# Local layers' output product: four f32 products per tile become twelve f32r products, attention's output being split beforehand

## The chip, the cores and the metric

One core of a Trainium2 chip runs the whole program. The metric is the device time of one execution in microseconds (us). Engines are named as the profile names them: PE is TensorE's matmul, PEld its weight loads, DVE is VectorE, ACT is ScalarE, POOL is GpSimd, SP is SyncE, which here only issues transfers.

## The reference, cut to what matters

A global attention over x (4 x 1024 tokens, 256 features, 16 heads) gives a gate. A second branch takes the normalised x through two layers of local attention and a gated feed-forward net; the two are multiplied and x is added. Of a local layer this case touches one line, `x = x + o  wo`:

```python
def _layer(x, wqkv, qs, ksc, wo, lg, lb, w1, b1, w2, b2):
    h = shift_token(x)
    q, k, v = jnp.split(h  wqkv, 3, axis=-1)
    ...
    o = local_attention(q, k, v)              # 8 heads of 64, windows of 128
    o = o.transpose(0, 2, 1, 3).reshape(b, n, INNER)   # INNER = 512
    x = x + o  wo                            # wo: 512 x 256 per layer
    h = shift_token(x)
    ...                                       # layer norm
    a, g = jnp.split(h  w1 + b1, 2, axis=-1)
    x = x + (a * gelu(g))  w2 + b2
    return x
```

## The kernel before

Three stages follow each other, with a barrier between them. `prepare_tokens` normalises x and makes the queries, keys and values of the global attention. `global_attention` works on 32 units; early in it SP also brings in what the local layers need: it copies the raw wqkv and w1 from DRAM to DRAM (`copy_raw`, L820 and L821), then issues `place_rows` (the row maxima that the first score products of the stage need, L437), then the small tables, `load_wo`, `load_w2`, waits for the raw copies, and issues `load_wqkv` and `load_w1`. `local_layers` is the long stage.

In `local_layers` the 4096 tokens are 8 chunks of 512 columns, each chunk four windows of 128. `body(g)` runs for g = 0 to 17 on every engine; the list `PLAN` fixes which layer's attention and which layer's feed-forward it does. In body(g), window w, the attention of chunk g is prepared (`project`, `rotate`), scored one window later and weighted with the values another window later, while the feed-forward net of chunk g - 2 goes on in parts between them. Bodies 0 and 1 have no feed-forward part; in its place they do the output projection of the global attention (`divide`, `project_o`, `take_s`). Bodies 3 to 7, 8 and 9, and 11 to 15 are hardware loops. Bodies 2 to 16 hold 15 output products and the last chunk's one is written out apart (`late_output`, in body 16). There is no scheduler: each engine executes its function in the order in which it is written, and semaphores alone tie them together. So the order around the change is that of the functions `body` of each engine.

What is touched: the output product (`output_product`, `late_output`) reads the attention's output from `o_ring` (two slots of 4 x 512 columns, f32) and the weights from `wo_l`, as f32 operands: 4 matmuls for each of the two output tiles m. `o_ring` is filled by ScalarE from the bank `l_ps_o` in `take_o` (L1474); a chunk's slot is complete after window 1 of the next body, and the product reads it in window 0 of the body after that. Other large products of the local layers already are f32r: their operands were split into a high part (rounded to f32r) and a low part (the remainder), and three products high x high, low x high, high x low stand for one (`THREE`). The feed-forward net's features are kept so in `f_high` and `f_low` (512 columns x 2 each), the projection's in `h`. `exponentials` (ScalarE) goes through the 8 heads of a window, four per half; `normalise` (VectorE, L1688) scales them; `add_ffn` (VectorE, L1774) empties the banks of the `down` product, ffn1 and then ffn0, which the next output product fills again, and `carry` (L1780) ends VectorE's part of a body. `scale_tables` (VectorE, L1888) multiplies a layer's rope tables by its scales: layer 0 ahead of body 0, layer 1 in window 1 of body 2.

## Time and profile before

| | |
|---|---|
| time, median of 3 runs | 2290.24 us (2288.89 to 2292.75) |
| the profiled execution's own time | 2290.47 us |
| its span in the trace | 2287.5 us |
| mean granted TensorE clock in it | 0.975 of full |
| PE busy | 2176.3 us (95%) |
| DVE busy | 1630.8 us (71%) |
| ACT busy | 1375.2 us (60%) |
| POOL busy | 614.8 us (27%) |

Busy time is the time in which an engine had an instruction under way. In the rows below, a body is named by its number, and a line is that of the kernel before. A row of the timeline gives the start, the duration and the instruction, and in square brackets how long its engine stood idle before it and who released it. An f32 matmul of 512 columns stands in the trace as two records, an f32r matmul as one: "x16" of the output product is 8 matmuls.

### The profile page before, as it was taken

Reading aid. Unit: us, or ns where it says so; the run is one execution under the profiler, and the core shown is the slowest. Engines: PE = TensorE matmul, PEld = TensorE weight load, DVE = VectorE, ACT = ScalarE, POOL = GpSimd, SP = SyncE. Lnnn points to the kernel's source line nnn. Section 1 sums busy time; section 2 is a strip of 40 time slices with the busy share of each in tenths; the row PEclk is TensorE's granted clock in tenths of the full one; section 3 lists DMA queues with packets and bytes.
Section 4 is the critical chain, followed back from the end, with each engine's and each line's share of the span. In section 5 each row is a group of like instructions: output and inputs, shape, how many; then the busy total and the mean of one; then the engine's idle time right before and its main releaser. Section 6 shows DMA issues by size and latency. Waiting matters only on the chain.

```text
span 2287.5 us, 43380 instructions
## 1 busy us (share of the span) xinstructions
PE 2176.3 (95%) x14560; PEld 1278.4 (56%) x14560; DVE 1630.8 (71%) x3801; ACT 1375.2 (60%) x2547; POOL 614.8 (27%) x493
## 2 busy tenths in 40 slices
PE   7869999999999988989999999999999999999998
PEld 4533333333333335656766766756766766766755
DVE  6668999999999936666666665656666666665645
ACT  2215888888888864645655655645655655655633
POOL 4421200000000005423333333323333333333302
PEclk9977999999999999999999999999999999999999
DMA  4485222112211122210000000000010000000122
GB/s 149 172 240 175 57 67 62 55 55 66 66 57 54 38 63 95 95 38 1 1 0 0 0 0 0 28 1 1 9 37 1 1 0 0 0 0 0 55 92 74
DMA packets 76983, 108.94 MB, mean 48 GB/s; under 512 B 14204, under 2 KB 49360, under 8 KB 76752
## 3 DMA queue, kind: packets, MB, share of 16 engines
q1 hardware_dynamic: 76864, 107.30, 14.9%
q8 instruction: 81, 1.33, 0.2%
q14 instruction: 38, 0.31, 0.0%
HBM read 68.74 MB, written 43.95 MB: 49 GB/s over the span
## 4 chain that ended last, share of the span: by engine, by line
PE 50%; DVE 2%; issue 2%; ACT 1%; DVEq 0%; ACTq 0%
PE ffn L1201 24%; PE l_ps_o L1159 5%; PE ring L1147 5%; PE ring L1187 4%; PE ps_v L1134 3%; PE ps_q L1134 3%; PE ring L1171 2%; PE ps_k L1134 2%; DVE l_probs L1676 1%; PE ring L1189 1%; PE ring L1190 0%; DVE l_probs L1688 0%; ACT k_ring L1482 0%; ACT l_probs L1490 0%; PE ps_k L1223 0%
## 5 line engine op out<-in xcount | busy, mean ns | idle before, releaser
L669 DVE TENSOR_REDUCE maxima<-ps_m 128x1 f32<-128x512 f32 x1024 | 629.3, 683 | 22.5 <-PE ps_m L549 18.2
L737 ACT ACTIVATE probs<-ps_st 128x1024 f32<-128x1024 f32 x512 | 521.0, 1024 | 163.8 <-PE ps_st L576 144.8
L549 PE MATMUL ps_m<-k_st,q_st 48*128 48x512 f32 x1024 | 394.0, 468 | 19.9 <-DMA k_st<-ks 15.8
L1490 ACT ACTIVATE l_probs<-l_probs,l_neg_max 128x256 f32<-128x256 f32 x512 | 254.0, 498 | 194.6 <-DVE l_neg_max L1676 194.6
L576 PE MATMUL ps_st<-q_st,k_st 50*128 50x512 f32 x1024 | 369.1, 445 | 1.2 <-DMA q_st<-max_rows 0.9
L592 PE MATMUL ps_o<-probs,v_st 128*32 128x256 f32 x4096 | 323.4, 394 | 0.1
L1676 DVE CUSTOM_DVE_ANT_1 l_probs<-ring,l_mask 128x256 f32<-128x256 f32 x384 | 140.0, 421 | 198.6 <-PE ring L1187 198.2
L576 PEld LDWEIGHTS ps_st<-q_st,k_st 50*128 50x128 f32 x1024 | 155.1, 187 | 194.4 <-issue 174.9
L1469 ACT COPY p_turned<-ring 128x512 f32<-128x512 f32 x256 | 140.5, 599 | 163.5 <-PE ring L1147 163.3
L1096 POOL TENSOR_SCALAR clipped<-sumsq 128x16 f32<-128x16 f32 x64 | 16.2, 253 | 767.4 <-DVE sumsq L1643 767.4
L549 PEld LDWEIGHTS ps_m<-k_st,q_st 48*128 48x128 f32 x1024 | 167.4, 191 | 53.3 <-DVE maxima L669 31.3
L1098 POOL TENSOR_TENSOR inv_norm<-clipped,halves 128x16 f32<-128x16 f32 x64 | 187.6, 2932 | 5.3
L592 PEld LDWEIGHTS ps_o<-probs,v_st 128*32 128x32 f32 x4096 | 84.3, 108 | 170.5 <-ACT probs L737 110.4
L1769 DVE SCALAR_TENSOR_TENSOR hidden<-ffn,b_l,gate 128x512 f32<-128x512 f32 x96 | 71.9, 749 | 144.0 <-PE ffn L1201 69.7
L1201 PE MATMUL ffn<-hidden,w_l 128*128 128x512 f32 x384 | 172.9, 600 | 0.0
L1688 DVE TENSOR_SCALAR l_probs<-l_probs,l_inv_total 128x256 f32<-128x256 f32 x512 | 166.3, 388 | 4.5
L1147 PE MATMUL ring<-l_ident,l_probs 128*128 128x128 f32 x1024 | 143.5, 281 | 14.4 <-DVE l_probs L1688 14.4
L1100 POOL TENSOR_TENSOR rope_a<-rope_a,rope_b 128x1024 f32<-128x1024 f32 x64 | 156.9, 2452 | 0.0
L1159 PE MATMUL l_ps_o<-p_turned,v_ring 128*64 128x128 f32 x2048 | 149.1, 283 | 4.6 <-ACT p_turned L1469 4.5
L508 POOL TENSOR_TENSOR max_hl<-row_max,zeros 128x16 fp32r<-128x16 f32 x32 | 7.1, 223 | 532.8 <-DVE row_max L678 532.8
L1159 PEld LDWEIGHTS l_ps_o<-p_turned,v_ring 128*64 128x64 f32 x2048 | 109.4, 137 | 65.6 <-issue 42.0
L1106 POOL TENSOR_TENSOR qk_n<-rope_a,inv_norm 128x1024 f32<-128x1024 f32 x64 | 123.2, 1926 | 72.7 <-PE ring L1171 62.4
(192 smaller groups left out, 3868.9 us busy)
## 6 DMA issues: line engine op xcount, KB each, us to landing
qs<-split SPq DMA_DIRECT2D x16, 512.0 KB, 3.5
ks<-split SPq DMA_DIRECT2D x16, 512.0 KB, 5.1
q_st<-qs SPq DMA_DIRECT2D x64, 128.0 KB, 2.6
k_st<-ks SPq DMA_DIRECT2D x64, 128.0 KB, 3.2
o<-o_sb SPq DMA_DIRECT2D x32, 256.0 KB, 2.5
hidden<-o SPq DMA_DIRECT2D x17, 256.0 KB, 6.1
x_in<-in_L_attn_x_dram SPq DMA_DIRECT2D x8, 512.0 KB, 5.6
v<-v_sb SPq DMA_DIRECT2D x16, 256.0 KB, 4.7
```

The lines of the kernel that those rows point to most:

```text
L549: nc.tensor.matmul(bank(base, use)[:, :], q_st[u][r, qt * P:(qt + 1) * P], k_st[u][r, h * CH:(h + 1) * CH], start=True, stop=True).then_in ...
L576: mm = nc.tensor.matmul(ps_st[j][:, h * CH:(h + 1) * CH], k_st[u][r, kt * P:(kt + 1) * P], q_st[u][r, h * CH:(h + 1) * CH], start=True, st ...
L592: mm = nc.tensor.matmul(ps_o[r:r + 32, q], v_st[:, kt, 2 * u + j, :], probs[:, kt % 4, j, h * CH + q.start:h * CH + q.stop], start=(kt == ...
L669: nc.vector.tensor_reduce(maxima[:, par, side(e), tile + e // 4, e % 2:e % 2 + 1], bank(base, k + e)[:, :], AX_X, ALU.max).then_inc(m_used, 1)
L737: nc.scalar.activation(probs[:, kt % 4, j, :], ps_st[j][:, :], ACT.Exp, scale=float(G_DIM) ** -0.5).then_inc(exp_done, 1)
L1098: nc.gpsimd.tensor_tensor(inv_norm[:, :], clipped[:, :], halves[:, :], ALU.pow).then_inc(inv_done, 1)
L1134: mm = nc.tensor.matmul(bank[:, :], h[a][:, k, w * P:(w + 1) * P], wt.wqkv[b][:, k, n * INNER:(n + 1) * INNER], start=(e == 0), stop=(e == ...
L1147: mm = nc.tensor.transpose(ring[(PT + p) % 2][:, (2 * j + s) * P:(2 * j + s + 1) * P], probs[:, 2 * p + j, s * P:(s + 1) * P], wt.ident[:, :])
L1159: mm = nc.tensor.matmul(ps_o[j * HDIM:(j + 1) * HDIM, p * P:(p + 1) * P], v_ring[:, slot, head * HDIM:(head + 1) * HDIM], p_turned[:, p % ...
L1201: mm = nc.tensor.matmul(ffn[bank][:, :], a, b, start=(n == 0), stop=(n == len(operands) - 1))
L1490: nc.scalar.activation(probs[:, head, :], probs[:, head, :], ACT.Exp, bias=neg_max[:, head:head + 1], scale=-1.0, accum_out=total[:, head: ...
L1688: ins = nc.vector.tensor_scalar(probs[:, head, :], probs[:, head, :], inv_total[:, head:head + 1], None, ALU.mult)
```

## The change

`wo` is held twice, high and low (f32r), and o_ring's room is shared with a new tile `o_low` (f32r) of the same size and place. In window 3 of body g (g = 1 to 15) ScalarE copies the slot that body g + 1 will multiply into `f_high` and `f_low`, which are free then: columns of heads 0 to 3 into f_high, 4 to 7 into f_low (`take_o_high`, 2 copies of 128 x 1024, between the two halves of the exponentials). GpSimd then subtracts that from o_ring, in place (`leave_o_low`, 2 operations of 128 x 1024). The output product takes 12 f32r matmuls per tile m in place of 4 f32 ones and waits for GpSimd (`o_split`) instead of ScalarE (`o_out`). For the last chunk the same is done in window 1 of body 16, into the tiles h.

The weights: SP copies wo raw from DRAM to DRAM too, ahead of `place_rows`, waits for three copies instead of two, and loads wo after w1. Ahead of bodies 2 and 10 ScalarE rounds wo into the high tile and VectorE subtracts; PE waits for that (`wo_low`) before the body's first product. For room, the `scales` now lie in `rope_a`, so both layers' tables are scaled ahead of body 0 and none in body 2.

```diff
 global_attention, sync
                 wt.copy_raw(sp)
                 place_rows(0, 0)
                 wt.load_small(nc, sp)
-                wt.load_wo(sp, 0)
                 wt.load_w2(sp, 0)
-                sp.wait_ge(wt.raw, 32)
+                sp.wait_ge(wt.raw, 48)
                 wt.load_wqkv(sp, 0)
                 wt.load_w1(sp, 0)
+                wt.load_wo(sp, 0)
...
+        sp.dma_start(self.wo_dram, self.dram["wo"]).then_inc(self.raw, 16)
...
-        scales = sb("scales", [P, DEPTH, 2, HDIM])
+        scales = rope_a[:, 0, 0:DEPTH * 2 * HDIM].rearrange("p (l s n) -> p l s n", l=DEPTH, s=2)
...
+        def o_high(g, p):
+            return features_of(g)[p // KD][:, p % KD, :]
+
+        def wo_products(g, m):
+            low = o_low[:, g % 2, :, :] if isinstance(g, int) else o_low[:, bass.ds(g % 2, 1), :, :].rearrange("p o h n -> p (o h) n")
+            cols = slice(m * P, (m + 1) * P)
+            return [(wt.wo[a][:, p, cols], low[:, p, :] if b else o_high(g, p)) for p in range(HEADS // 2) for a, b in ((0, 0), (1, 0), (0, 1))]
...
+                if weights and weights[0] == "w1" and prepare:
+                    prepare("wo", weights[1])
 gpsimd
+                def leave_o_low(g):
+                    pool.wait_ge(o_high_done, g - 1)
+                    slot = (lambda x: x[:, g % 2, :, :]) if isinstance(g, int) else (lambda x: x[:, bass.ds(g % 2, 1), :, :].rearrange("p o h n -> p (o h) n"))
+                    for p in range(0, HEADS // 2, KD):
+                        ins = nc.gpsimd.tensor_tensor(slot(o_low)[:, p:p + KD, :], slot(o_ring)[:, p:p + KD, :], features_of(g)[p // KD][:, :, :], ALU.subtract)
+                    ins.then_inc(o_split, 1)
...
+                        if isinstance(g, int) and g == LAST and w == 1:
+                            leave_o_low(g + 1)
...
+                        if w == 3 and not (isinstance(g, int) and g == 0):
+                            leave_o_low(g + 1)
 tensor
                 def output_product(g, lf):
-                    pe.wait_ge(o_out, WPC * (g - 1))
+                    pe.wait_ge(o_split, g - 1)
                     for m in range(KD):
-                        ffn_fill(g, m, WO, [(wt.wo[:, p, m * P:(m + 1) * P], o_ring[:, bass.ds(g % 2, 1), p, :].rearrange("p o n -> p (o n)"))
-                                            for p in range(HEADS // 2)])
+                        ffn_fill(g, m, WO, wo_products(g, m))
...
                         if w == 0 and before_hidden:
-                            pe.wait_ge(wt.wo_in, 16 * (lf + 1))
+                            pe.wait_ge(wt.wo_low, lf + 1)
 scalar
+                def take_o_high(g):
+                    act.wait_ge(o_out, WPC * (g - 1))
...
+                    for p in range(0, HEADS // 2, KD):
+                        ins = nc.scalar.copy(features_of(g)[p // KD][:, :, :], slot[:, p:p + KD, :])
+                    ins.then_inc(o_high_done, 1)
...
                         if mid_:
-                            exponentials(W)
+                            exponentials(W, (lambda: take_o_high(g + 1)) if split_next else None)
+                        if isinstance(g, int) and g == LAST and w == 1:
+                            take_o_high(g + 1)
...
+                    if name == "wo":
+                        act.wait_ge(wt.wo_in, 16 * (l + 1))
+                        nc.scalar.copy(wt.wo[0][:, :, :], wt.wo[1][:, :, :].bitcast(F32)).then_inc(wt.wo_high, 1)
+                        return
 vector
+                    if name == "wo":
+                        dve.wait_ge(wt.wo_high, l + 1)
+                        nc.vector.tensor_tensor(wt.wo[1][:, :, :], wt.wo[1][:, :, :].bitcast(F32), wt.wo[0][:, :, :], ALU.subtract).then_inc(wt.wo_low, 1)
+                        return
                     if l == 0:
-                        scale_tables(0 if name == "wqkv" else 1)
+                        if name == "wqkv":
+                            for layer in range(DEPTH):
+                                scale_tables(layer)
                         return
```

What stands on the engines, in the order of the compiled programs. PE, the loop of bodies 3 to 7, start of the output product in window 0, before (line 1201; ISA and REGISTER_ALU rows compute an address or a wait's value):

```order
L1245 ISA
L1197 ISA [waits o_out]
L1201 ISA [waits ffn_taken0]
L1201 MATMUL ffn<-o_ring,wo_l 128x512
L1201 ISA
L1201 MATMUL ffn<-o_ring,wo_l 128x512
L1201 ISA
L1201 MATMUL ffn<-o_ring,wo_l 128x512
L1201 ISA
```

The same place now (line 1233):

```order
L1277 REGISTER_ALU
L1229 ISA [waits o_split]
L1233 MATMUL ffn<-f_high,wo_high 128x512 [waits ffn_taken0]
L1233 MATMUL ffn<-f_high,wo_low 128x512
L1233 ISA
L1233 MATMUL ffn<-o_low,wo_high 128x512
L1233 MATMUL ffn<-f_high,wo_high 128x512
L1233 MATMUL ffn<-f_high,wo_low 128x512
L1233 ISA
```

The product keeps its place between the turned probabilities and the values. Its wait is for GpSimd's signal now, and a tile's 4 matmuls are 12, with four address computations still among the first tile's.

ACT, same loop, window 3, now (line 1534 is that of the exponentials, 1523 that of the new copies): the last three of the first half's four exponentials, then the copies.

```order
L1534 ACTIVATE l_probs,l_total<-l_probs,l_neg_max 128x256
L1534 ACTIVATE l_probs,l_total<-l_probs,l_neg_max 128x256 [waits ring_taken1]
L1534 ACTIVATE l_probs,l_total<-l_probs,l_neg_max 128x256
L1523 ISA [waits o_out]
L1523 COPY f_high<-o_ring 128x1024
L1523 ISA
L1523 COPY f_low<-o_ring 128x1024
L1533 REGISTER_ALU
```

The second half's exponentials, which followed the first half's directly, now come behind both copies.

And POOL, same loop, window 3, now: the sum and the multiplication of the window (lines 1130 and 1136), then the subtractions (1113).

```order
L1130 TENSOR_TENSOR rope_a<-rope_a,rope_b 128x1024
...
L1136 TENSOR_TENSOR qk_n<-rope_a,inv_norm 128x1024 [waits ring_ready1]
L1113 ISA [waits o_high_done]
L1113 TENSOR_TENSOR o_low<-o_ring,f_high 128x1024
L1113 ISA
L1113 TENSOR_TENSOR o_low<-o_ring,f_low 128x1024
L1081 REGISTER_ALU
```

Before, the loop ended behind the multiplication into qk_n; the two subtractions are new there.

## Rows read from the trace of the kernel before

**Rows 1.** The page: the span.
```profile
span 2287.5 us, 43380 instructions
```
**Rows 2.** Busy by stretch, body 5: length; PE, PEld, DVE, ACT, POOL; granted clock.
```profile
1251.40:1335.30 83.90, 82.89 (x489) 56.51 (x489) 53.29 (x153) 48.47 (x119) 30.08 (x16) 1.00 0.00 0
```
**Rows 3.** The chain that ended last, 1228 to 1320: start, us, what.
```profile
1251.40 6.87 PE ffn L1201 x16
...
1312.58 2.81 PE ffn L1201 x12
```
**Rows 4.** Timeline, 1228 to 1290: window 3 of body 4 into body 5.
```profile
1243.37 0.51 ACT L1490 ACTIVATE l_probs<-l_probs,l_neg_max 128x256 f32<-128x256 f32 x1 [3.95 <-DVE l_neg_max L1676]
...
1245.69 1.14 DVE L1688 TENSOR_SCALAR l_probs<-l_probs,l_inv_total 128x256 f32<-128x256 f32 x4
...
1247.77 0.75 DVE L1774 SCALAR_TENSOR_TENSOR xnt<-ffn,b_l,mid 128x512 f32 x1 [0.28 <-PE ffn L1201]
...
1251.23 7.03 PE L1201 MATMUL ffn<-o_ring,wo_l 128*128 x16
```
**Rows 5.** Timelines of POOL and of DVE around 1286, window 1 of body 5.
```profile
1285.48 1.91 POOL L1106 TENSOR_TENSOR qk_n<-rope_a,inv_norm 128x1024 f32<-128x1024 f32 x1 [0.23 <-POOL rope_a L1100]
...
1285.78 2.55 DVE L1688 TENSOR_SCALAR l_probs<-l_probs,l_inv_total 128x256 f32<-128x256 f32 x4
```
**Rows 6.** Groups by line and form: busy us, mean ns.
```profile
L870 POOL TENSOR_TENSOR wqkv_low<-wqkv_low,wqkv_high 128x1536 fp32r<-128x1536 f32 x2 | 6.9, 3474 | 0.2
...
L1610 ACT CAST wqkv_high<-wqkv_low 128x1536 fp32r<-128x1536 f32 x2 | 2.8, 1460 | 0.0
```
**Rows 7.** Transfers by line: KB each, us from issue to landing.
```profile
w_raw<-in_L_ffn_w_dram SPq DMA_DIRECT2D x1, 2728.0 KB, 21.5
```
**Rows 8.** Timeline, 160 to 212: the first score product of the global stage.
```profile
184.74 0.79 PE L576 MATMUL ps_st<-q_st,k_st 50*128 50x512 f32 x1 [0.87 <-DMA q_st<-max_rows]
```
**Rows 9.** Timeline, 832 to 860: start of the local stage.
```profile
851.97 2.63 DVE L1888 TENSOR_TENSOR tables<-tables,scales 128x512 f32<-128x512 f32 x6 [4.58 <-DMA scales<-in_L_ffn_k_scale_dram]
...
858.56 0.60 PE L1134 MATMUL ps_q<-wqkv_high,h_high 128*128 128x512 f32 x1 [4.58 <-DVE rope_b L1648]
```
**Rows 10.** Timeline, 972 to 987: window 3 of body 1.
```profile
984.80 1.22 DVE L1655 TENSOR_TENSOR mid<-hidden 128x1024 f32<-128x1024 f32 x1
...
986.08 1.22 PE L1284 MATMUL ffn<-mid,dev 128*128 128x512 f32 x1 [5.74 <-DVE mid L1655]
```
**Rows 11.** Timeline of PE, 990 to 1032: body 2's start and its window 1.
```profile
993.39 0.47 PE L1134 MATMUL ps_q<-wqkv_high,h_high 128*128 128x512 f32 x1 [0.72 <-issue]
...
1030.83 0.50 PE L1189 MATMUL ring<-k_ring,q_t 64*128 64x128 f32 x4 [1.87 <-DVE l_neg_max L1676]
```
**Rows 12.** Timeline, 1493 to 1512: body 7 into body 8.
```profile
1500.94 3.43 DVE L1877 TENSOR_TENSOR wqkv_low<-wqkv_low,wqkv_high 128x1536 fp32r<-128x1536 f32 x2
...
1504.70 0.79 PE L1134 MATMUL ps_q<-wqkv_high,h_high 128*128 128x512 f32 x1 [5.17 <-DVE wqkv_low L1877]
...
1511.24 1.02 PE L1201 MATMUL ffn<-o_ring,wo_l 128*128 x2
```
**Rows 13.** Timelines of PE and DVE, 1668 to 1680: body 9 into body 10.
```profile
1675.04 0.79 PE L1134 MATMUL ps_q<-wqkv_high,h_high 128*128 128x512 f32 x1
...
1676.89 0.23 DVE L1780 TENSOR_SCALAR xnt<-xnt,parity  x1 [0.50 <-DVE xnt L1774]
...
1679.11 1.45 PE L1201 MATMUL ffn<-o_ring,wo_l 128*128 128x512 f32 x3
```
**Rows 14.** Timeline of PE, 2186 to 2287: body 16.
```profile
2203.84 1.97 PE L1147 MATMUL ring<-l_ident,l_probs 128*128 128x128 f32 x8 [2.42 <-DVE l_probs L1688]
...
2214.67 0.40 PE L1201 MATMUL ffn<-f_high,w_high 128*128 128x512 f32 x1
```
**Rows 15.** Busy by stretch, same columns: the two us behind that wait.
```profile
2204.00:2206.00 2.00, 1.81 (x8) 1.41 (x8) 1.77 (x8) 1.97 (x5) 0.00 (x0) 0.50 0.00 0
```
**Rows 16.** Timeline of ACT, 2196 to 2287: body 16, windows 1 and 2.
```profile
2213.78 0.69 ACT L1534 ACTIVATE gate<-ffn,b_l 128x512 f32<-128x512 f32 x1
```

More of the change, by code:

```diff
@@ L783, in __init__ @@
         self.w1 = [sb(f"w1_{n}", [P, KD, (2 * FT + 1) * P], F32R) for n in ("high", "low")]
-        self.wo = sb("wo_l", [P, INNER // P, D])
+        self.wo = [sb(f"wo_{n}", [P, INNER // P, D], F32R) for n in ("high", "low")]
         self.w2 = sb("w2_l", [P, FT + 1, D])
@@ L797, in __init__ @@
         self.w1_dram = nc.dram_tensor("w1_raw", (DEPTH, D, 2 * HID), F32, kind="Internal").ap()
+        self.wo_dram = nc.dram_tensor("wo_raw", (DEPTH, INNER, D), F32, kind="Internal").ap()
         self.raw = sem("raw")
@@ L800, in __init__ @@
         self.w1_high, self.w1_low = sem("w1_high"), sem("w1_low")
+        self.wo_high, self.wo_low = sem("wo_high"), sem("wo_low")
         self.set = sem("w_set")
@@ L914, in local_layers @@
         p_turned = sb("p_turned", [P, 2, 2, 2, P])
-        o_ring = sb("o_ring", [P, 2, HEADS // 2, CH])
+        with nc.sbuf_tensor("o_ring", [P, 2, HEADS // 2, CH], F32) as o_ring:
+            pass
+        o_low = sb("o_low", [P, 2, HEADS // 2, CH], F32R)
         mid = sb("mid", [P, KD, 1 + CH])
@@ L957, in local_layers @@
         sq_dev = sem("sq_dev")
+        o_high_done, o_split = sem("o_high_done"), sem("o_split")
         mid_summed = sem("mid_summed")
@@ L1227, in late_output @@
                     g = LAST + 1
-                    pe.wait_ge(o_out, WPC * (g - 1))
+                    pe.wait_ge(o_split, g - 1)
                     pe.wait_ge(roped, WPC * LAST)
                     for m in range(KD):
-                        late_fill(m, [(wt.wo[:, p, m * P:(m + 1) * P], o_ring[:, g % 2, p, :]) for p in range(HEADS // 2)])
+                        late_fill(m, wo_products(g, m))
                 def late_mean():
@@ L1243, in output_product @@
                 def output_product(g, lf):
[L1245 removed]
+                    pe.wait_ge(o_split, g - 1)
                     for m in range(KD):
[L1247 to L1248 removed]
+                        ffn_fill(g, m, WO, wo_products(g, m))
                 def mean(g):
@@ L1482, in take_qk, with exponentials @@
                     nc.scalar.copy(k_ring[:, :, ws * P:(ws + 1) * P], ring[TK % 2][:, :].rearrange("p (h n) -> p h n", n=P)).then_inc(ring_taken[TK % 2], 1)
-                def exponentials(W):
+                def take_o_high(g):
+                    act.wait_ge(o_out, WPC * (g - 1))
+                    if late(g):
+                        act.wait_ge(v_mm, WPC * LAST)
+                    slot = o_ring[:, g % 2, :, :] if isinstance(g, int) else o_ring[:, bass.ds(g % 2, 1), :, :].rearrange("p o h n -> p (o h) n")
+                    for p in range(0, HEADS // 2, KD):
+                        ins = nc.scalar.copy(features_of(g)[p // KD][:, :, :], slot[:, p:p + KD, :])
+                    ins.then_inc(o_high_done, 1)
+                def exponentials(W, between=None):
                     for n in range(HEADS):
+                        if n == HEADS // 2 and between:
+                            between()
                         head = scored(n)
@@ L1583, in body @@
                             take_s(W - 1)
+                        split_next = w == 3 and not (isinstance(g, int) and (g == 0 or g >= LAST))
                         if mid_:
-                            exponentials(W)
+                            exponentials(W, (lambda: take_o_high(g + 1)) if split_next else None)
+                        if isinstance(g, int) and g == LAST and w == 1:
+                            take_o_high(g + 1)
                         if not forward and W == CHUNKS - 1:
```

5 lines of the change are left out of this document (2 added, 3 removed).

## Prediction

> **What bounds the kernel now.** I read the page first: a span of 2287.5 us [rows 1]. The profiled execution's own time, 2290.47 us, is 2.97 more, and 0.23 above the median 2290.24. The sum below is made against 2290.47. Next, busy time by stretch: in one body of the steady part, 83.90 us long, PE is busy for 82.89, DVE for 53.29, ACT for 48.47 and POOL for 30.08, at full granted clock [rows 2]. The reader should see that PE is the bound there and that the others have room, though not at every moment. Then the chain that ended last: in the steady bodies it stays on PE, an output product takes 6.87 us in it and a hidden tile of 12 f32r matmuls 2.81 [rows 3]. Last, the timelines of the places where PE does stand idle, because there the bound is another engine: the starts of the stages [rows 8, 9], the end of body 1 [rows 10], body 8's start [rows 12], body 16 [rows 14].
>
> **The gain.** One f32r matmul of this size costs 2.81 / 12 = 0.234 us [rows 3]. The new product has 24 of them: 5.62 us in place of 6.87, 1.25 saved. There are 15 output products and the late one: 16 x 1.25 = 20.0 us, all of it PE time. PE is at full clock around nearly all of them.
>
> **The steady border (bodies 3 and up), costed at nothing.** ScalarE's two copies: a cast of 1536 columns takes 1.46 us [rows 6], so 1024 take 0.97 and both 1.95. They stand where ACT idles for 3.95 us until VectorE's maxima of the second half [rows 4]; with that cover gone they would cost 1.95 a border. GpSimd's two subtractions: the only row of that form gives 3.47 us for 1536 columns [rows 6], so 2.31 each, 4.63 together. They start when the copies end, at about 1241.4, and end at 1246.0 to 1246.5. Is VectorE free meanwhile? In window 1 of body 5 a group of four `normalise` operations, begun while POOL ran qk_n until 1287.39, took 2.55 us instead of 1.14 [rows 4, 5]. So I hold VectorE's operations that touch SBUF alone until GpSimd's instruction ends; without that hold the sum below would be 5.8 us lower (2.4 in c, 1.7 in e, 1.7 in f). The Trainium skill (page "SBUF — State Buffer", section "SBUF: two separate sides") has this as a rule that speaks against the change: GpSimd and VectorE share a port pair that whoever starts first locks for its whole instruction. By that rule, the trace agrees: the whole excess of the row is one stay until qk_n's end, and a mere sharing of bandwidth would have the sum near the lower one. With the hold, both groups of normalise end at about 1248.9 where the second ended at 1246.8, and `add_ffn` of bank ffn0, before 1247.77 + 0.75 = 1248.5, ends at about 1250.4. The output product needs that bank at 1251.23 [rows 4]: 0.9 us are left, so I charge nothing. `carry` comes 1.7 later, and it only matters where something behind it is awaited (below). Queued behind PE's new wait for `o_split` are the whole window's products, but GpSimd is done 4.7 us before it.
>
> **The losses, in order of time.**
> a. The raw copy of wo, 1024 KB, is ahead of `place_rows` in SP's queue. The raw copies of wqkv (2 x 256 x 1536 x 4 bytes = 3072 KB) and of w1 (2728 KB) are in after 21.5 us [rows 7], so 1024 KB more take at most 21.5 x 1024 / 5800 = 3.8 us. PE's first score product waits for the transfer that `place_rows` makes [rows 8]. Other transfers share those 21.5 us, so I take +3.0 (0, if the rows pass beside the copies, to 3.8). The load of wo, moved behind w1, lands long before the local stage.
> b. Layer 1's tables are scaled ahead of body 0 too: VectorE's 2.63 us [rows 9] lie straight on the path to `rope_b` and PE's 4.58 of idle. +2.65. In body 2's window 1 they go, and with them PE's wait of 1.87 for VectorE's maxima [rows 11]: -1.9.
> c. End of body 1. ACT's exponentials of the two halves are back to back here (no wait between them), so the copies push the second half back by 1.95; the last ended at 983.4. The subtractions run from about 983.3 to 987.9 and hold normalise and `divide` (1.22 us, from 984.80), for which PE stands idle until 986.08 [rows 10]. Divide would end at 987.9 + 1.14 + 1.22 = 990.3 against 986.0: +4.4 (2.0, if GpSimd holds nothing, to 4.6).
> d. Body 2's start. PE waits for `wo_low` before its first product: ScalarE, once done with the last `take_s` (about when PE starts), rounds wo in 0.97, VectorE subtracts in 3.43 / 2 x 2 / 3 = 1.15 [rows 12], 0.15 of signals: +2.25, since PE now goes on at once [rows 11]. What does an idle of that kind do to the clock? After 2.42 us of idle at 2203.84 the granted clock was 0.50, the level of 1.2 GHz [rows 14, 15]. After body 8's 5.17 the way from the first product to the output product took 6.54 us, against 4.07 in body 10: 2.5 lost [rows 12, 13]. Bounds 0 and 3.4; an idle of 2.25 is nearest to the 2.42, but short: +1.5.
> e. Body 8's start hangs on VectorE: carry, then 3.43 us for wqkv, then PE [rows 12]. Carry 1.7 later: +1.7 (0 to 2.3).
> f. Body 10's start. Before, PE went on at 1675.04. Now it waits until carry (1677.12), 1.15 of subtraction and 0.15 of signal are over, 1678.4: +3.4. Carry's delay adds 1.7 (0 to 2.3), and the clock 2.4 as at body 8 (0 to 2.9) [rows 12, 13]. Together +7.5.
> g. Body 16. The copies for the last chunk stand ahead of ACT's gate 0 (2213.78 to 2214.47) [rows 16], whose bank PE refills at 2214.67 [rows 14]: 1.95 later, +1.85. An idle of that length may lower the clock: +0.8 (0 to 1.7). The subtractions are done long before the late product.
>
> Sum: 3.0 + 0.75 + 4.4 + 3.75 + 1.7 + 7.5 + 2.65 = 23.75; less 20.0, +3.75: 2294.2 us, 2294.0 against the median.
>
> **The rivals.**
> Faster: GpSimd does not hold VectorE here, and the clock does not fall. For it: VectorE may slip in between GpSimd's two instructions, and the idles of d and g are shorter than any behind which my rows show a fallen clock. Against it: [rows 5, 12, 15]. The terms c, e and f lose 2.4, 1.7 and 1.7, the clock 1.5, 2.4 and 0.8: 10.5 less, 2283.7, or 2283.5 against the median.
> Slower: the border is dearer than I think, so that ffn0 comes free after PE asks for it. It decides from 0.9 us on: if the copies take 1.4 us each, or a subtraction 2.8, every one of some 13 borders stalls. With a stall of 0.7 us each, +9: about 2303. For it: my 2.31 is scaled from an instruction outside the loop, and the slack is the smallest in the argument. Against it: POOL's sum over 1024 columns takes about the same (qk_n 1.91 [rows 5]).
> The change does not do what it says: the f32r product is no faster, because the address computations that stand between the first tile's matmuls stop the flow, as an f32 matmul's length hid them. At 0.06 to 0.25 us for each of four, in 12 looped products, +3 to +12: 2297 to 2306, say 2300 (with four times 0.12). Against it: the hidden tiles run at 0.234 though they too are in the loops, but with few such computations between.
>
> **How the numbers follow.** The forecast case, terms near my values, has 0.52; its own range is 2289.5 to 2298.5, from the two or three terms that can be off at once. Faster has 0.20, the slow border 0.13, the stopped flow 0.07; 0.08 stays for what I have not seen, half to each side. The measurement tells some 0.2% (4.6 us) from no change, so faster is below 2285.7 and slower above 2294.8. My case is half under and half over the upper bound with most of its weight under it (0.34 to 0.18); so faster 0.20 + 0.04, slower 0.13 + 0.07 + 0.18 + 0.02, same 0.36. The range 2283 to 2302 reaches into the faster case and to the slow border, leaving about a tenth at either end.
>
> **What would show it.** In the profile after: an output product of 24 matmuls in 5.6 us in the chain (a product above 6 means the flow is stopped); POOL's new operations near 2.31 and ACT's copies near 0.97; the normalise groups of window 3 twice as long as 1.14; no idle of PE before the output product, by ffn0's release. PE idle of about 5 us before the first products of bodies 2 (2.2) and 10 (5), half the clock behind them; at the global stage's start a first score product 3 us later, counted from the stage's barrier; project_o's last wait near 10 us. I would be wrong by the largest amount if body 10's start costs only its 3.4, or if each border stalls a little: the number of borders multiplies whatever I have missed there.

## The result, and the profile after

The changed kernel takes 2306.99 us (median of 5 runs, 2305.39 to 2315.7), the kernel before 2289.68 us beside it (5 runs, 2287.88 to 2292.75). The ratio on record is 1.0065, 95% interval 1.0046 to 1.0084; the quotient of the two medians, 1.0076, lies inside it. The change makes the kernel slower, by 13 us more than forecast (2294.0), and the time lies above the range (2283 to 2302).

The page of the changed kernel: the span grew by 17.6 us, though PE has 15 us less to do (2161.2 us of busy time against 2176.3 in the table above).

```profile
span 2305.1 us, 43754 instructions
...
PE 2161.2 (94%) x14688; PEld 1303.6 (57%) x14688; DVE 1673.2 (73%) x3803; ACT 1406.7 (61%) x2581; POOL 689.3 (30%) x525
```

Where is the difference? The starts of a body's first PE product in both traces give it stage by stage (body 0 by its window 1):

| | before | after | behind | grown by |
|---|---|---|---|---|
| first score product, global stage | 184.74 | 189.16 | 4.42 | 4.42 |
| last score product of that stage | 840.27 | 844.59 | 4.32 | -0.10 |
| body 0, window 1 | 858.56 | 865.82 | 7.26 | 2.94 |
| body 1 | 914.75 | 922.24 | 7.49 | 0.23 |
| body 2 | 993.39 | 1006.84 | 13.45 | 5.96 |
| body 3 | 1079.29 | 1091.30 | 12.01 | -1.44 |
| body 7 | 1415.03 | 1426.23 | 11.20 | -0.81 |
| body 8 | 1504.70 | 1517.02 | 12.32 | 1.12 |
| body 9 | 1591.10 | 1602.34 | 11.24 | -1.08 |
| body 10 | 1675.04 | 1690.73 | 15.69 | 4.45 |
| body 11 | 1762.95 | 1780.25 | 17.30 | 1.61 |
| body 15 | 2098.70 | 2115.50 | 16.80 | -0.50 |
| last instruction of DVE | 2283.50 | 2301.01 | 17.51 | 0.71 |

The steps up at the edges are there much as forecast. What is missing are the steps down: bodies 3 to 6 and 11 to 14 should have gained 1.25 us each and gained 0.8 and 0.5 in four together.

So I looked into one steady body. PE's timeline of the changed kernel, body 5:

```profile
1262.61 0.48 PE L1233 MATMUL ffn<-f_high,wo_high 128*128 128x512 f32 x1
...
1268.34 1.09 PE L1191 MATMUL l_ps_o<-p_turned,v_ring 128*64 128x128 f32 x16
1269.37 1.09 PE L1179 MATMUL ring<-l_ident,l_probs 128*128 128x128 f32 x8
1271.40 1.10 PE L1233 MATMUL ffn<-hidden,mean_w 128*128 128x512 f32 x2 [0.94 <-issue]
```

The product is as short as forecast: from its start to the next step 5.73 us (1262.61 to 1268.34), where it took 6.96 (1251.23 [rows 4] to 1258.19, below). There is no wait ahead of it in this body. But three steps on, before the product that forms the mean of `mid`, PE is idle for 0.94 us. "Issue" hides the releaser; the mean's operand is VectorE's sum (L1782), so I read VectorE next, same kernel and place:

```profile
1255.60 3.00 DVE L1739 TENSOR_SCALAR l_probs<-l_probs,l_inv_total 128x256 f32<-128x256 f32 x4
...
1259.79 1.40 DVE L1825 SCALAR_TENSOR_TENSOR xnt<-ffn,b_l,mid 128x512 f32 x2
...
1268.56 0.69 DVE L1756 TENSOR_TENSOR mid<-ffn,xnt 128x512 f32<-128x512 f32 x1 [1.07 <-PE ffn L1233]
1269.35 1.95 DVE L1782 TENSOR_TENSOR hidden<-mid 128x512 f32<-128x512 f32 x1
```

And GpSimd:

```profile
1253.00 2.36 POOL L1113 TENSOR_TENSOR o_low<-o_ring,f_high 128x1024 f32 x1 [2.17 <-ACT f_low L1523]
1255.31 2.36 POOL L1113 TENSOR_TENSOR o_low<-o_ring,f_low 128x1024 f32 x1
1265.15 0.25 POOL L1126 TENSOR_SCALAR clipped<-sumsq 128x16 f32<-128x16 f32 x1 [7.48 <-DVE sumsq L1694]
...
1268.39 2.37 POOL L1130 TENSOR_TENSOR rope_a<-rope_a,rope_b 128x1024 f32<-128x1024 f32 x1
```

The sum takes 1.95 us, and it ends 0.54 us after GpSimd's addition does (1270.76), a little less than the 0.69 us that it takes when it runs freely. The same three instructions in the timeline of the kernel before, and the step behind its output product:

```profile
1256.55 2.35 POOL L1100 TENSOR_TENSOR rope_a<-rope_a,rope_b 128x1024 f32<-128x1024 f32 x1
...
1258.19 1.09 PE L1159 MATMUL l_ps_o<-p_turned,v_ring 128*64 128x128 f32 x16
1259.21 0.69 DVE L1731 TENSOR_TENSOR hidden<-mid 128x512 f32<-128x512 f32 x1
...
1260.15 1.02 PE L1201 MATMUL ffn<-hidden,mean_w 128*128 128x512 f32 x2
```

There the addition ended at 1258.90 and the sum began 0.31 us later, untouched. The reader should see that 0.31 us: it was all the room between the two. The output product, now 1.3 us shorter, brings the sum forward by as much, into the addition.

Bodies 2 to 15 all show it, in two sizes. In bodies 4 to 7, 9 and 12 to 15 GpSimd's addition also begins 0.38 to 0.55 us later, counted from the body's start, than before, and PE's idle ahead of the mean is 0.94 to 1.11 us. In bodies 3 and 11 the addition begins 9.39 us after the start, as it did before; the sum then takes 1.56 us and the idle is 0.56 us (in bodies 2, 8 and 10 it is 0.56 to 0.61). Body 3, which begins at 1091.30:

```profile
1100.69 2.37 POOL L1130 TENSOR_TENSOR rope_a<-rope_a,rope_b 128x1024 f32<-128x1024 f32 x1
...
1102.04 1.56 DVE L1782 TENSOR_TENSOR hidden<-mid 128x512 f32<-128x512 f32 x1
...
1103.71 1.10 PE L1233 MATMUL ffn<-hidden,mean_w 128*128 128x512 f32 x2 [0.56 <-issue]
```

Over the 14 bodies this idle adds up to 12.1 us; the kernel before has none there.

The other main places where PE idles in the changed kernel, one for each of the terms a to g, in their order, and between f and g one more, for which the prediction has no term:

```profile
189.16 0.79 PE L576 MATMUL ps_st<-q_st,k_st 50*128 50x512 f32 x1 [4.86 <-DMA q_st<-max_rows]
...
865.82 0.80 PE L1166 MATMUL ps_q<-wqkv_high,h_high 128*128 128x512 f32 x1 [7.51 <-DVE rope_b L1699]
...
997.54 2.93 PE L1315 MATMUL ffn<-mid,dev 128*128 128x512 f32 x3 [9.70 <-DVE mid L1706]
...
1006.84 0.80 PE L1166 MATMUL ps_q<-wqkv_high,h_high 128*128 128x512 f32 x1 [2.88 <-DVE wo_low L1923]
...
1517.02 0.79 PE L1166 MATMUL ps_q<-wqkv_high,h_high 128*128 128x512 f32 x1 [6.40 <-DVE wqkv_low L1934]
...
1690.73 0.80 PE L1166 MATMUL ps_q<-wqkv_high,h_high 128*128 128x512 f32 x1 [3.98 <-DVE wo_low L1923]
...
2202.12 0.47 PE L1233 MATMUL ffn<-f_high,wo_high 128*128 128x512 f32 x1 [1.29 <-DVE xnt L1825]
...
2233.41 0.50 PE L1233 MATMUL ffn<-f_high,w_high 128*128 128x512 f32 x1 [1.71 <-ACT gate L1578]
```

The row at 2202.12 is body 16's output product. PE has no new chunk to project ahead of it there, comes to it early, and waits for `add_ffn` (L1825) to empty the bank. The kernel before shows no such wait in body 16; all kernels below that hold the change show one of 1.28 or 1.29 us.

### The profile page after: what moved, and what is told of

Same layout as the page of the kernel before. It is cut to its first block and busy times, and to the rows that moved or that the text cites. A ratio compares the mean times of both kernels' runs of the same rounds, so it can differ in the third digit from the quotient of the medians.

```text
span 2305.1 us, 43754 instructions
## 1 busy us (share of the span) xinstructions
PE 2161.2 (94%) x14688; PEld 1303.6 (57%) x14688; DVE 1673.2 (73%) x3803; ACT 1406.7 (61%) x2581; POOL 689.3 (30%) x525
## 3 DMA queue, kind: packets, MB, share of 16 engines
q8 instruction: 82, 1.34, 0.3%
## 5 line engine op out<-in xcount | busy, mean ns | idle before, releaser
L737 ACT ACTIVATE probs<-ps_st 128x1024 f32<-128x1024 f32 x512 | 520.8, 1024 | 167.9 <-PE ps_st L576 148.6
L1739 DVE TENSOR_SCALAR l_probs<-l_probs,l_inv_total 128x256 f32<-128x256 f32 x512 | 193.9, 441 | 4.5
```

The source lines that it names most:

```text
L737: nc.scalar.activation(probs[:, kt % 4, j, :], ps_st[j][:, :], ACT.Exp, scale=float(G_DIM) ** -0.5).then_inc(exp_done, 1)
L1739: ins = nc.vector.tensor_scalar(probs[:, head, :], probs[:, head, :], inv_total[:, head:head + 1], None, ALU.mult)
```

## The experiments

Ten kernels, on two groups of questions: what takes the gain of the steady bodies, and what the edges cost. Beside them the kernel before was timed on the same chip, with medians of 2293 to 2294 us. Between the traces most of the difference that no edit explains arises in one place: at the start of the global stage the granted clock rises from 0.50 to full at different moments. In the stretch 200 to 230 us it was 0.53 on the mean in wait_late and 1.00 in raw_later, and that stage then lasted 663.6 and 652.8 us from its first to its last score product. So the steady bodies are compared by their period in the traces, the distance from the first product of body 5 to that of body 6; in a trace it repeats from body 4 to body 6 within 0.15 us.

**pool_waits.** GpSimd's addition behind VectorE's sum, in window 0.

```diff
                         pool.wait_ge(roped, W + 1)
+                        if w == 0 and lf is not None:
+                            pool.wait_ge(mid_summed, g - 1)
                         nc.gpsimd.tensor_tensor(rope_a
```

> The changed kernel, but GpSimd starts the addition of the rotated parts in window 0 (L1130) only after VectorE's sum for the mean (L1782). In the changed kernel that sum took 1.95 us in body 5, ending about when the addition does, and PE then stood idle 0.94 us before the mean's product; PE was 1.31 us ahead of the old schedule before that product and 1.10 of it was gone after. Theory (GpSimd's addition holds VectorE's sum, and the shorter output product brings the sum into it): the sum takes 0.69 us again, the idle goes, and each of 13 bodies gains 1.0 to 1.25 us: 13 to 16 us less than the changed kernel's 2307, 2291 to 2294. Rival (the sum is late for another reason, the delay of VectorE at the border or the product's own end): the sum stays near 1.95 us or PE waits as long, and the time stays within 3 us of 2307. GpSimd's later addition should cost nothing, as it waits 3.9 us for PE's turn behind it.

Measured: 2297.57 us (10 runs), ratio to the kernel before 1.0004 (0.9984 to 1.0024). The period fell from 83.80 to 82.64, 1.16 us. VectorE and GpSimd in body 5:

```profile
1273.19 0.69 DVE L1758 TENSOR_TENSOR mid<-ffn,xnt 128x512 f32<-128x512 f32 x1 [1.06 <-PE ffn L1235]
1273.99 0.69 DVE L1784 TENSOR_TENSOR hidden<-mid 128x512 f32<-128x512 f32 x1
...
1274.76 2.36 POOL L1132 TENSOR_TENSOR rope_a<-rope_a,rope_b 128x1024 f32<-128x1024 f32 x1 [1.70 <-DVE hidden L1784]
```

The sum takes 0.69 us as soon as the addition is not beside it, and PE goes on to the mean at once. The addition, 1.7 us later, costs nothing that the period shows. The theory holds; the time in us stands above the expected 2291 to 2294, but the kernel before, timed beside it, took 2293.55 us, 3.9 more than beside the changed kernel. By the ratios, 1.0004 against 1.0065, the wait gives back some 0.6%, 14 us.

**mean_later.** The same stall, covered instead of removed.

```diff
-                        if forward and w == 0 and not late(g):
-                            mean(g)
...
                             values(W, w, 3)
+                        if forward and w == 0 and not late(g):
+                            mean(g)
```

> The changed kernel, but PE does the mean's product behind the last two products with the values of window 0 (1.03 us of work) in place of ahead of them; GpSimd and VectorE keep their order. Theory (PE waits only for the sum, held by GpSimd until its addition ends): the sum still takes about 1.95 us, but PE's idle of 0.94 before the mean is filled, and 0.9 to 1.0 us a body are gained in 13 bodies, some 12 us: about 2295. Rival (the whole chain behind the mean, centring, squares, variance, has no room, so that the stall only moves): PE idles later in the window, and the time stays within 3 us of 2307.

Measured: 2299.13 us (10 runs), ratio 1.0009 (0.9981 to 1.0037); period 83.06, 0.74 us less than the changed kernel's, where 0.9 to 1.0 was expected, and 0.42 us more than with pool_waits. The sum still takes 1.95 us in its median, and PE no longer waits for it. So most of what PE lost was the wait for the sum. Part of the rest is a new wait, for ScalarE's copy of the turned probabilities, ahead of the products that were moved forward:

```profile
1277.71 1.15 PE L1191 MATMUL l_ps_o<-p_turned,v_ring 128*64 128x128 f32 x16 [0.24 <-ACT p_turned L1500]
```

The other 0.2 us is not accounted for.

**before_short.** The kernel before with a shorter output product and nothing of the change.

```diff
-                                            for p in range(HEADS // 2)])
+                                            for p in range(HEADS // 2 - 1)])
```

> The kernel before, with one of the four f32 matmuls of each output tile left out (its output leaves out heads 6 and 7 in the output product). No operation of the change is in it. An output product is 6.87 / 4 = 1.72 us shorter. Theory (a shorter output product alone brings VectorE's sum into GpSimd's addition, which ends 11.7 us after the body's start whatever PE does): the sum waits for it, takes up to about 2 us, and PE is only 0.3 to 0.6 us ahead per body behind the mean; the time falls by 16 x 0.3 to 0.6, 5 to 10 us below the kernel before. Rival (the copies and subtractions of the change are what makes VectorE or GpSimd late): without them the full 1.72 us a product comes through, 16 x 1.72 = 27 us below the kernel before.

Measured: 2281.85 us (10 runs), ratio 0.9952 (0.9934 to 0.9969). The period is 83.42 against 83.94: of 1.72 us taken off PE, 0.52 arrive. Body 5's start in its timeline:

```profile
1263.77 2.36 POOL L1100 TENSOR_TENSOR rope_a<-rope_a,rope_b 128x1024 f32<-128x1024 f32 x1
...
1263.92 0.69 DVE L1705 TENSOR_TENSOR mid<-ffn,xnt 128x512 f32<-128x512 f32 x1 [1.04 <-PE ffn L1201]
1264.72 1.96 DVE L1731 TENSOR_TENSOR hidden<-mid 128x512 f32<-128x512 f32 x1
...
1266.79 1.10 PE L1201 MATMUL ffn<-hidden,mean_w 128*128 128x512 f32 x2 [0.95 <-issue]
```

No copy, no subtraction, no f32r product: the shorter product alone brings the sum into the addition. The rival, that the stall needs the change's own operations, is out. (This product is 1.72 us shorter, not 1.31, so the sum begins 0.95 us into the addition, and the idle is as long as in the changed kernel's later additions. How much of the changed kernel's own stall comes from the shorter product alone is read from its bodies 3 and 11: 0.56 us. The time is 11.7 us below the kernel before, where the expectation had 5 to 10; 3.7 of them arise behind body 15's start.) The first DVE row is worth a look too: the addition to `mid`, which reads a PSUM bank, ran 0.69 us beside GpSimd, unheld.

**short_waits.** before_short with the wait of pool_waits.

```diff
-                                            for p in range(HEADS // 2)])
+                                            for p in range(HEADS // 2 - 1)])
...
+                        if w == 0 and lf is not None:
+                            pool.wait_ge(mid_summed, g - 1)
```

> The kernel before with one of four f32 matmuls of each output tile left out (heads 6 and 7 are missing from the output product, as in before_short) and GpSimd's addition of window 0 behind VectorE's sum. Nothing of the change is in it. Theory: what the shorter product gave back in before_short (period 83.43 instead of 83.94, 0.51 of 1.72 us) comes through: period 82.2 to 82.3, and 13 to 15 us less than before_short, 1.1 to 1.2% below the kernel before. Rival (the stall behind the shorter product has a second cause): the period stays above 82.8.

Measured: 2266.52 us (4 runs), ratio 0.9876 (0.9848 to 0.9905). The period is 82.23: the 1.72 us arrive whole (1.71), and there is no second cause behind the first. GpSimd's wait by itself gains nothing either, or more than 1.72 would have arrived.

**add_halves.** Is it a hold, or do the two engines share a rate?

```diff
-                        nc.gpsimd.tensor_tensor(rope_a[:, :, :], rope_a[:, :, :], rope_b[:, :, :], ALU.add).then_inc(added, 1)
+                        for s in range(2):
+                            ins = nc.gpsimd.tensor_tensor(rope_a[:, s, :], rope_a[:, s, :], rope_b[:, s, :], ALU.add)
+                        ins.then_inc(added, 1)
```

> The changed kernel, but GpSimd's addition of the rotated parts is two instructions of 512 columns in place of one of 1024, in every window. It tells what is held and for how long. Theory (VectorE's instruction on SBUF alone stands still until the GpSimd instruction under way ends): VectorE's sum for the mean, begun 0.9 to 1.0 us into the addition, is let in at the first half's end, some 0.3 us later, and takes 0.9 to 1.2 us instead of 1.95; GpSimd's second half then starts later or beside it; PE's idle before the mean falls from 0.94 to 0.1 or less, and a looped body takes 82.7 to 83.1 instead of 83.8 to 83.95 us. Rival (the two engines only share the rate): the sum still takes 1.8 to 2.0 us, since the same amount of GpSimd's work lies beside it, and the bodies keep their period.

Measured: 2297.9 us in one run; the period is 82.87 in place of 83.80. The timeline of body 5:

```profile
1265.90 1.27 POOL L1131 TENSOR_TENSOR rope_a<-rope_a,rope_b 128x512 f32<-128x512 f32 x1
...
1267.13 1.72 POOL L1131 TENSOR_TENSOR rope_a<-rope_a,rope_b 128x512 f32<-128x512 f32 x1
...
1266.86 0.86 DVE L1784 TENSOR_TENSOR hidden<-mid 128x512 f32<-128x512 f32 x1
...
1267.82 1.10 PE L1235 MATMUL ffn<-hidden,mean_w 128*128 128x512 f32 x2
```

The sum began 0.96 us into the first half and took 0.86 us, a little below the expected 0.9. It ended 0.55 us after the first half's end (1267.17), as in the changed kernel it ends 0.54 us after the whole addition's. The second half took 1.72 us where the first took 1.27, so now GpSimd waited for VectorE. A shared rate would have left the sum near 1.95.

Body 3 of the same trace is the other side of it. There the sum begins 0.1 us behind the start of the second half, and waits that half out:

```profile
1098.82 2.50 POOL L1131 TENSOR_TENSOR rope_a<-rope_a,rope_b 128x512 f32<-128x512 f32 x2
...
1100.18 1.70 DVE L1784 TENSOR_TENSOR hidden<-mid 128x512 f32<-128x512 f32 x1
```

It takes 1.70 us, more than the 1.56 beside the undivided addition, and body 3 is no shorter (83.73 us against 83.45). So an instruction is the unit of the hold: cutting it in two frees the other engine if that engine comes during the first half, and gains nothing if it comes during the second.

**raw_later.** The raw copy behind the row maxima.

```diff
-        sp.dma_start(self.wo_dram, self.dram["wo"]).then_inc(self.raw, 16)
...
                 place_rows(0, 0)
+                sp.dma_start(wt.wo_dram, wt.dram["wo"]).then_inc(wt.raw, 16)
                 wt.load_small(nc, sp)
```

> The changed kernel, but the raw copy of wo is issued behind the transfer of the row maxima (place_rows) instead of ahead of it. Theory (the copy delays that transfer, for which PE idles 4.86 us at 189.16 against 0.87 before): the idle goes back to about 0.9 us and the time is 4 us lower, about 2303. Rival (the idle is due to something else, or the copy then delays a later transfer of the stage): the global stage ends as late as in the changed kernel, 2307.

Measured: 2305.42 us (6 runs, 2299.92 to 2325.85), ratio 1.0074 (1.0037 to 1.0112). PE at the first score product:

```profile
186.73 0.79 PE L577 MATMUL ps_st<-q_st,k_st 50*128 50x512 f32 x1 [1.69 <-DMA q_st<-max_rows]
```

The idle of 4.86 us is 1.69. Is that all that the copy costs? The kernels that have no copy of wo ahead of the row maxima show how far this idle scatters by itself: 0.87 in the kernel before, 1.22 in short_waits, 1.66 in edges, 1.14 in all_fixed, and in before_short, whose global stage is that of the kernel before:

```profile
185.71 0.79 PE L576 MATMUL ps_st<-q_st,k_st 50*128 50x512 f32 x1 [1.74 <-DMA q_st<-max_rows]
```

With the copy ahead it is 4.42 to 5.69 in six traces. So 1.69 is the idle without the copy's cost, and the cost is 2.7 to 4.8 us. The time does not show the gain (2303 was expected, and the ratio is no lower than the changed kernel's 1.0065): this stage's start is where the clock's rise scatters the runs by more.

**wait_late.** PE waits for wo where it reads it.

```diff
-                        if w == 0 and before_hidden:
-                            pe.wait_ge(wt.wo_low, lf + 1)
...
+                        if w == 0 and before_hidden:
+                            pe.wait_ge(wt.wo_low, lf + 1)
                         if forward and w == 0 and not late(g):
                             output_product(g, lf)
```

> The changed kernel, but in bodies 2 and 10 PE waits for the split wo right ahead of the output product, its first reader, and no longer ahead of the body's first product, some 4 us earlier. Theory (the whole loss at body 10's start is PE's idle for wo_low and the slower clock behind it): the idle of 2.88 at body 2 shrinks to about 0.7 and the 3.98 at body 10 goes, the clock behind them stays at full, so that body 9 takes about 84 instead of 88.4 us from start to start and body 10 about 88 instead of 89.5; together 6 to 8 us: about 2300. Rival (VectorE's subtraction and the held carry are late for the rest of the body's start as well): the idle turns up at the output product or behind it, and less than 3 us are gained. The clock's part: if it falls all the same, behind body 9's end or the wait in body 10's window 1 (2.11), body 10 keeps its 89.5.

Measured: 2296.89 us (10 runs), ratio 1.0019 (1.0001 to 1.0038). From body to body it takes, against the changed kernel: body 1, 81.90 (84.60); body 2, 83.10 (84.46); body 9, 83.88 (88.39); body 10, 88.55 (89.52). Together 9.5 us, more than the 6 to 8 expected. The clock is part of it. The stretches by busy time, six us at the starts of bodies 2 and 10 (the figure behind the five engines is the granted clock), of the changed kernel:

```profile
1006.00:1012.00 6.00, 5.16 (x21) 4.26 (x22) 1.68 (x4) 1.29 (x3) 0.00 (x0) 0.72 0.12 47
1690.00:1696.00 6.00, 5.27 (x13) 4.04 (x14) 1.50 (x3) 0.60 (x1) 0.00 (x0) 0.50 0.14 47
```

and of wait_late:

```profile
1011.00:1017.00 6.00, 5.33 (x28) 4.37 (x28) 3.54 (x5) 3.69 (x6) 0.00 (x0) 1.00 0.21 87
1688.00:1694.00 6.00, 5.84 (x26) 3.82 (x24) 5.47 (x13) 2.42 (x5) 0.67 (x1) 1.00 0.34 102
```

PE idled 2.88 and 3.98 us ahead of the first two stretches, and 0.68 us ahead of the third; ahead of the fourth there was no wait. Two waits appear later in body 10, a small one at the output product and one in window 1:

```profile
1694.16 0.50 PE L1233 MATMUL ffn<-f_high,wo_high 128*128 128x512 f32 x1 [0.32 <-DVE wo_low L1923]
...
1719.12 0.66 PE L1191 MATMUL l_ps_o<-p_turned,v_ring 128*64 128x128 f32 x8 [2.11 <-ACT p_turned L1500]
```

The second also stands in the kernel before, and is gone in the changed kernel, where the body starts late. So body 10 gains only 1.0 us here, although the clock at its start stays at 1.00; behind the second wait it falls to 0.50 for some 3 us, as it does in the kernel before.

**body1.** The end of body 1.

```diff
+                    if isinstance(g, int) and g == 2:
+                        pool.wait_ge(divided, CHUNKS)
...
-                            exponentials(W, (lambda: take_o_high(g + 1)) if split_next else None)
+                            exponentials(W, (lambda: take_o_high(g + 1)) if split_next and forward else None)
+                        if split_next and not forward:
+                            take_o_high(g + 1)
```

> The changed kernel, but in window 3 of body 1 ScalarE's two copies stand behind both halves of the exponentials, and GpSimd's two subtractions wait for VectorE's last division. Theory (copies and subtractions delay the division, for which PE idles 9.70 us there against 5.74 before): the idle goes back to 5.7, and body 2 starts 4.0 us earlier, counted from body 1's start (80.6 instead of 84.6 us, the rest being the wait for wo). Rival (the division is late because VectorE is held by something else, or the subtractions, now later, delay body 2's output product): the distance from body 1's start to body 3's stays at 169 us.

Measured: 2306.59 us in one run. PE's wait for the division, 9.70 us, is 5.72:

```profile
996.15 4.64 PE L1317 MATMUL ffn<-mid,dev 128*128 128x512 f32 x5 [5.72 <-DVE mid L1710]
```

and body 1 takes 80.95 in place of 84.60. From body 1's start to body 3's it is 165.56 instead of 169.06: 3.5 us gained and kept.

**edges.** The edits at the edges undone (what the steady border does to body 8's start, term e, stays): wait_late, body1, and

```diff
-        scales = rope_a[:, 0, 0:DEPTH * 2 * HDIM].rearrange("p (l s n) -> p l s n", l=DEPTH, s=2)
+        scales = o_ring[:, 1, 0, 0:DEPTH * 2 * HDIM].rearrange("p (l s n) -> p l s n", l=DEPTH, s=2)
...
-                            for layer in range(DEPTH):
-                                scale_tables(layer)
+                            scale_tables(0)
...
+                        if isinstance(g, int) and g == 0 and w == 1:
+                            scale_tables(1)
...
-                wt.load_wo(sp, 0)
+                sp.dma_start(wt.wo_dram, wt.dram["wo"]).then_inc(wt.raw, 16)
...
+                            if isinstance(g, int) and g == LAST:
+                                take_o_high(g + 1)
```

> The changed kernel with all edits at the edges of the stages undone and the steady border left as it is: the wait for wo and body 1 as in the two kernels above; the raw copy of wo at the end of SP's issues in the global stage and its load at the local stage's start; layer 1's tables scaled at the end of body 0's window 1, with the scales in a free part of o_ring; body 16's copies behind the first gate. Theory: global stage +0, local start 2.7 us less, body 1 4.0, bodies 2 and 10 some 6 to 8, body 16 up to 1, raw copy 4: 18 to 20 less than the changed kernel, 2287 to 2289, no more than 0.1% below the kernel before, since the 14 output products still give back 1.1 us each to the wait before the mean. Rival (the edges were dearer or cheaper in the sum than in the traces, for instance through the clock): above 2293 or below 2283.

Measured: 2289.63 us (12 runs), ratio 0.9985 (0.9968 to 1.0001). As the theory had it: about 0.15% under the kernel before and hardly to be told from it, 0.6 us above the 2287 to 2289 expected. By the ratios, 0.9985 against 1.0065, it is 0.8% or 18 us below the changed kernel. The losses that these edits undo are paid back and the output products bring next to nothing; the period is 83.81. Term e is still there: body 7 takes 90.77 us from start to start, against 89.67 before.

**all_fixed.** edges and pool_waits together.

> The kernel with all edges undone, and GpSimd's addition of window 0 behind VectorE's sum for the mean in the looped bodies. Theory (the two groups of losses add up, and only the output product's gain is left): 14 x 1.15 = 16 us below the kernel with the edges alone, 2270 to 2274, 0.7 to 0.9% below the kernel before. Rival (bodies that now run early meet other waits at the border, such as VectorE's held normalise at the bank of the output product): body periods above 82.9 instead of 82.64, and a time above 2278.

Measured: 2272.78 us (6 runs, 2268.63 to 2276.34), ratio 0.9908 (0.9884 to 0.9933). Its page:

```profile
span 2272.9 us, 43769 instructions
```

PE's timeline at the starts of bodies 5 and 6:

```profile
1247.66 0.79 PE L1169 MATMUL ps_q<-wqkv_high,h_high 128*128 128x512 f32 x1
...
1330.26 0.79 PE L1169 MATMUL ps_q<-wqkv_high,h_high 128*128 128x512 f32 x1
```

A period of 82.60 us: 1.34 less than in the kernel before. The two groups of losses add up, and without them the change is worth 0.9% (0.7 to 1.2), about the 20 us that its products save on PE.

## Why the prediction was wrong

**The gain** was sized right on PE: 1.25 forecast, 1.31 measured from the body's start to the end of the output product (1258.62 to 1268.34 against 1247.16 to 1258.19).

**The step that failed** is the steady border, "costed at nothing". I asked which of the new operations could delay PE up to the output product, found 0.9 us of room at the bank ffn0, and stopped. That room was there in bodies 2 to 15: no wait stands ahead of the product. In body 16 it was not, and PE lost 1.29 us. But I did not ask what becomes early. With PE faster by 1.3 us in the middle of a body, everything behind the output product comes forward with it, except what GpSimd does at its own pace; and the first thing behind it on VectorE, the sum, had 0.31 us to the addition. PE stood idle there for 0.56 to 1.11 us in each of 14 bodies, 12.1 us in all, and taking the collision away gave back 14 us (pool_waits). That is nearly all of the 13 us between forecast and result; body 16's 1.29 us and edges that came out some 2 us cheaper than forecast make up the rest. before_short shows that a collision needs none of the change's operations, pool_waits and add_halves that it is GpSimd's instruction that holds the sum. I had the rule and the row for that hold in hand and used it only around the new instructions. The rival "slower" came near the time (2303, an equal stall at each border) by luck: it named another place and a cause that occurred in body 16 alone. Subtractions took 2.36 and copies 1.03 us, near my 2.31 and 0.97.

A smaller part is the border's own delay. The first group of normalise, begun 0.29 us into the second subtraction, took 3.00 us instead of 1.14, until 0.93 us after that subtraction's end; the second group took its 1.14, where I had expected both to be twice as long. `carry` began 3.00 us after the body's start instead of 1.78, VectorE's `sumsq` 5.13 instead of 4.75, and GpSimd's addition 9.77 instead of 9.39. Those 0.38 us, up to 0.55 in other bodies, are the difference between an idle of 0.56 us (bodies 3 and 11) and one of 0.94 to 1.11. So of the 12.1 us some 4 come from the copies and subtractions and some 8 from the shorter product alone. That split is read from the traces; no run took the border's delay away by itself.

**The losses at the edges**, forecast and measured:

| | forecast | measured, and from what |
|---|---|---|
| a, raw copy | 3.0 | 4.0: PE's idle 4.86 against 0.87 |
| b, tables | 2.65, then -1.9 | 2.9: 7.51 against 4.58; the 1.87 in body 2 is gone |
| c, end of body 1 | 4.4 (its own figures give 4.3) | 4.0: 9.70 against 5.74 |
| d, body 2 | 2.25 + 1.5 | 2.2 (2.88 against 0.72), and 1.4 behind it, with the clock at 0.72 for 6 us (84.46 against 83.10 in wait_late) |
| e, body 8 | 1.7 | 1.2: 6.40 against 5.17 |
| f, body 10 | 7.5 | 6.1: bodies 9 and 10 grew by 4.45 and 1.61, what their own products gained taken off |
| g, body 16 | 1.85 + 0.8 | 1.9 from body 15's start to that product, with an idle of 1.71 where there was none; the clock behind it stayed at 1.00 |

None is far off, and together they came out some 2 us below the forecast; a alone lies just above its bound (3.8). In f I left out that PE's wait of 2.10 us for ScalarE in body 10's window 1 would be covered when the body starts late:

```profile
1703.91 0.66 PE L1159 MATMUL l_ps_o<-p_turned,v_ring 128*64 128x128 f32 x8 [2.10 <-ACT p_turned L1469]
```

This is the kernel before; the changed kernel has no wait there, and wait_late has it again. That the address computations would stop PE's flow, the third rival, is out: in the loop 24 matmuls take 5.73 us, 0.24 each. The 0.06 to 0.25 us that I put on each of them came from no row, and no run shows such a price. That GpSimd doesn't hold VectorE, the faster rival, is out too. The fall of the clock was right as a mechanism for the longer idles: 0.50 and 0.72 behind 3.98 and 2.88, and 1.00 when these idles went (wait_late); behind the 1.71 us of g it did not fall, and behind the 2.1 us in body 10's window 1 it fell in the kernel before and in wait_late, not in pool_waits.

What stays open: what decides when the clock rises in the global stage, and why the idle before the first score product scatters from 0.87 to 1.74 us without the copy.

## What to carry to other kernels

When a product on the bounding engine gets shorter, list what is released behind it and look at what each of those instructions will now run beside; a gap of a few tenths of a us in the old trace is a warning, however idle the engine looks on average. The Trainium skill (page "SBUF — State Buffer", section "SBUF: two separate sides") says that GpSimd's and VectorE's shared port pair is taken for a whole instruction; the runs here agree (0.69 us became 1.95 beside a GpSimd instruction of 2.36, and 0.86 beside two of half the size), so GpSimd's long instructions are best placed, by a wait of their own, behind the VectorE instruction that PE wants next. And let the bounding engine wait for an operand at its first reader, not at the start of the block: here that alone was worth 9.5 us.

## What the runs showed of the hardware

Which of VectorE's instructions GpSimd holds: the sum (two operands in SBUF) and normalise (one tensor operand, in SBUF; in the changed kernel 4 of them, begun at 1255.60, took 3.00 us instead of 1.14 beside a subtraction that ended at 1257.67) stood still; the addition to `mid`, with one operand in PSUM, took its 0.69 us beside the same GpSimd instruction (before_short, 1263.92 beside 1263.77 to 1266.13). In the other direction, with VectorE's sum let in between GpSimd's two halves, the second took 1.72 us where the first took 1.27 (add_halves). A sum held by GpSimd ended 0.54 us after the instruction that held it, 0.15 less than its 0.69 alone; in the kernel before, normalise had 1.61 us of GpSimd's multiplication ahead of it and took 1.41 longer [rows 5].
